# The last pair's row sums of each batch: 32 columns wide, spread by transfers that ACT issues

## The reference

```
xn = group_norm(x)                        # 32 groups
q, k, v = split(w_qkv @ xn + b_qkv)       # 8 heads of 64 channels, 1024 positions
weight = softmax(q.T @ k / sqrt(64))      # over the 1024 keys
a = weight @ v
out = x + w_proj @ a + b_proj
```

## Time and profile before

| | |
|---|---|
| median of 3 runs | 2465.75 us (2464.68 to 2466.75) |
| the profiled execution's own time | 2465.66 us |
| its span | 2464.1 us |
| busy: PE, DVE, ACT, POOL | 2429.1, 1617.7, 1152.5, 1182.9 us |
| granted TensorE clock, mean | 0.994 of full speed |

### The profile page before, as it was taken

One profiled execution on the slowest core, in us unless ns is written; L12 is line 12 of the kernel. 1 busy time (PEld: TensorE's weight loads), 2 busy tenths in 40 slices (PEclk: granted clock), 3 DMA queues, 4 the chain that ended last, 5 costly groups with the idle time before them and its releaser, 6 DMA issues.

```text
span 2464.1 us, 37575 instructions
## 1 busy us (share of the span) xinstructions
PE 2429.1 (99%) x12980; PEld 1611.7 (65%) x12980; DVE 1617.7 (66%) x2164; ACT 1152.5 (47%) x1499; POOL 1182.9 (48%) x590
## 2 busy tenths in 40 slices
PE   8999999999899999999999999999999999999999
PEld 7878888788665566557556655755575566557555
DVE  7555555455566765775677577567756775775677
ACT  3322233223355644654555556456545554562554
POOL 3330000000047665773775567557737666672674
PEclk8999999999899999999999999999999999999999
DMA  6331110112231332315022312422151223222121
GB/s 201 133 113 41 68 68 35 50 51 84 113 112 35 112 128 95 120 35 214 31 98 98 142 36 110 177 71 102 28 213 35 104 100 131 78 69 103 35 69 44
DMA packets 73978, 226.76 MB, mean 92 GB/s; under 512 B 12288, under 2 KB 12288, under 8 KB 72960
## 3 DMA queue, kind: packets, MB, share of 16 engines
q1 hardware_dynamic: 59296, 172.01, 19.8%
q0 software_dynamic: 14560, 52.96, 5.9%
HBM read 141.05 MB, written 71.30 MB: 86 GB/s over the span
## 4 chain that ended last, share of the span: by engine, by line
PE 94%; DVE 3%; POOL 1%; issue 1%; ACT 1%; DMA 0%; ACTq 0%; SPq 0%; DVEq 0%; POOLq 0%
PE psum L1611 18%; PE psum L1551 15%; PE psum L1592 14%; PE psum L1364 11%; PE psum L1383 7%; PE psum L1562 7%; PE psum L1732 7%; PE psum L1407 4%; PE psum L1435 3%; PE psum L1630 2%; PE psum L1481 2%; POOL a_all L612 1%; PE psum L1375 1%; PE psum L1651 1%; PE psum L1495 1%
## 5 line engine op out<-in xcount | busy, mean ns | idle before, releaser
L612 POOL TENSOR_TENSOR a_all<-a_all 128x1024 f32<-128x1024 f32 x410 | 1011.3, 2467 | 496.2 <-ACT a_all L843 461.3
L843 ACT ACTIVATE a_all<-psum 128x1024 f32<-128x1024 f32 x512 | 496.5, 1021 | 79.7 <-PE psum L1592 65.5
L1146 DVE TENSOR_REDUCE small<-psum 128x2 f32<-128x1024 f32 x326 | 398.9, 1226 | 166.8 <-PE psum L1562 166.6
L1611 PE MATMUL psum<-a_all 128*64 128x512 f32 x2048 | 495.7, 605 | 0.0
L1592 PE MATMUL psum<-r_all 64*128 64x512 f32 x3200 | 415.6, 392 | 3.5 <-ACT a_all L843 2.0
L1551 PE MATMUL psum<-r_all 128*128 128x512 f32 x1536 | 364.1, 396 | 4.5 <-DVE r_all L1263 4.5
L1592 PEld LDWEIGHTS psum<-r_all 64*128 64x128 f32 x3200 | 299.8, 185 | 73.2 <-ACT a_all L843 14.0
L1551 PEld LDWEIGHTS psum<-r_all 128*128 128x128 f32 x1536 | 285.5, 189 | 85.1 <-issue 23.3
L1364 PE MATMUL psum<-r_all 128*128 128x512 f32 x1152 | 277.1, 396 | 1.1
L1611 PEld LDWEIGHTS psum<-a_all 128*64 128x64 f32 x2048 | 124.0, 136 | 232.8 <-issue 173.3
L1364 PEld LDWEIGHTS psum<-r_all 128*128 128x128 f32 x1152 | 213.1, 188 | 64.3 <-DVE r_all L1013 10.2
(11 more groups left out here) (157 smaller groups left out, 2613.0 us busy)
## 6 DMA issues: line engine op xcount, KB each, us to landing
r_all<-w_dram SPq DMA_DIRECT2D x48, 1024.0 KB, 4.9
xn_dram<-a_all POOLq DMA_DIRECT2D x56, 512.0 KB, 7.0
r_all<-xn_dram SPq DMA_DIRECT2D x7, 4096.0 KB, 15.4
a_all<-x SPq DMA_DIRECT2D x16, 1024.0 KB, 6.2
y_dram<-a_all SPq DMA_DIRECT2D x16, 1024.0 KB, 4.2
a_all<-y_dram SPq DMA_DIRECT2D x8, 2048.0 KB, 10.8
out<-a_all SPq DMA_DIRECT2D x28, 512.0 KB, 4.1
a_all<-sums SPq DMA_DIRECT2D x192, 64.0 KB, 2.0
```

What stands on the lines that cost most here:

```text
L612: pool.tensor_tensor(to, probs[:, 0, :, cols] if i == 1 else to, probs[:, i % SLOTS, :, cols], ALU.add).then_inc(sum_step, 1)
L843: act.activation(probs[:, i % SLOTS, :, cols], psum[half][:, :, :], ACT.Exp, scale=SCALE).then_inc(probs_ready, 1)
L1146: dve.reduce_max(max2[:, :, tile, half], of[:, :, :], AX_X).then_inc(work_free, 2)
L1611: last = pe.matmul(psum[2][h * D:(h + 1) * D, half], v_t[:, i, head], probs[:, i % SLOTS, h, half * HALF:(half + 1) * HALF], start=(i == 0 ...
```

## The change

The last pair of a batch (of the first seven) goes the way of the other pairs, with two differences. The quarters go to the first bank of psum[1], and the copy stands ahead of the staged row on ACT. And the eight transfers are issued by ACT, on its own queue (`spread_last`), where ACT before had no DMA. Counts of `recip_spread` and `quarters_inverted` now run over four pairs a batch. On DVE the four pieces of reciprocals stand after v tiles 1 and 2, in place of eight after tiles 1 to 4. `normalise` of the last pair waits for the transfers. PE's sums stay between v tiles 1 and 2. The eighth batch's last pair keeps the wide form.

```diff
         def spreads(b, p):
-            return b * (PAIRS - 1) + p
+            return b * PAIRS + p
...
                 act.wait_ge(sums_full, ONE + pairs + 1)
-                if p == PAIRS - 1:
-                    act.wait_ge(o_normed, NORMED0 + pairs * NH)
-                    act.activation(recip, of, ACT.Copy).then_inc(sums_copied, 1)
-                else:
-                    act.wait_ge(recip_spread, ONE + spreads(b, p) * SPREAD)
-                    act.activation(sums4, of, ACT.Copy).then_inc(sums_copied, 1)
+                act.wait_ge(recip_spread, ONE + spreads(b, p) * SPREAD)
+                act.activation(sums4, of, ACT.Copy).then_inc(sums_copied, 1)
+
+            def spread_last(b):
+                p = PAIRS - 1
+                act.wait_ge(quarters_inverted, (spreads(b, p) + 1) * CT)
+                act.wait_ge(o_normed, NORMED0 + (b * PAIRS + p) * NH)
+                for k in range(2 * NH):
+                    for r in range(2):
+                        at = k // NH * D + r * QUARTER
+                        act.dma_start(recip[at:at + QUARTER, k % NH], sums4[k * QUARTER:(k + 1) * QUARTER]).then_inc(recip_spread, 16)
...
                 if not last:
                     for h in range(NH):
                         hid_hi(b, PAIRS - 2, h)
+                    copy_sums(b, PAIRS - 1, psum[1][:, 0])
...
                 else:
-                    copy_sums(b, PAIRS - 1, psum[1][:, :, :])
+                    spread_last(b)
                 for h in range(NH):
                     hid_hi(b, PAIRS - 1, h)
...
                 for piece in range(first, first + n):
-                    if p == PAIRS - 1:
-                        part = recip[:, piece // CT, piece % CT * P:(piece % CT + 1) * P]
-                        dve.reciprocal(part, part).then_inc(sums_inverted, 1)
-                    else:
-                        part = sums4[:, piece * P:(piece + 1) * P]
-                        dve.reciprocal(part, part).then_inc(quarters_inverted, 1)
+                    part = sums4[:, piece * P:(piece + 1) * P]
+                    dve.reciprocal(part, part).then_inc(quarters_inverted, 1)
...
-                if p == PAIRS - 1:
-                    dve.wait_ge(sums_inverted, b * PIECES + (h + 1) * CT)
+                if end:
+                    dve.wait_ge(sums_inverted, h + 1)
                 elif h == 0:
                     dve.wait_ge(recip_spread, ONE + (spreads(b, p) + 1) * SPREAD)
...
-                        if 1 <= i <= 4:
+                        if i in (1, 2):
                             invert_sums(b, PAIRS - 1, 2 * (i - 1), 2)
...
                         if i == 1:
-                            sums(b * PAIRS + PAIRS - 1)
+                            sums(b * PAIRS + PAIRS - 1, psum[1][:, 0])
```

More of the change, by code:

```diff
@@ L321, in build @@
         ADDS = 2 * (NT - 1) - 1
-        PIECES = 2 * CT
         QUARTER = D // 2
@@ L1201, in invert_last, with normalise @@
                     dve.wait_ge(o_normed, NORMED0 + pairs * NH)
-                dve.reciprocal(recip[:, h], psum[1][:, h]).then_inc(sums_inverted, CT)
-            def normalise(b, p, h):
+                dve.reciprocal(recip[:, h], psum[1][:, h]).then_inc(sums_inverted, 1)
+            def normalise(b, p, h, end=False):
                 pairs = b * PAIRS + p
@@ L1327, in batch1 @@
                         invert_last(h)
-                        normalise(b, PAIRS - 1, h)
+                        normalise(b, PAIRS - 1, h, True)
                         hid_lo(b, PAIRS - 1, h)
```

## The result

| | before | after |
|---|---|---|
| median of 5 runs, us | 2464.72 (2464.56 to 2466.75) | 2480.38 (2477.22 to 2483.01) |
| ratio | | 1.0061, 95% interval 1.0049 to 1.0072 |
| profiled execution, us | 2465.66 | 2483.01 (span 2481.5) |

The kernel became slower by 15.7 us, 0.6%. The forecast was 2464.1 with a range to 2471: wrong, and outside its range.

What follows compares the result with a forecast made beforehand. PE's own queue was taken to bound the kernel (94% of the chain). The profiled 2465.66 us less PE's 1.7, other parts costing nothing, gave 2464.0, stated as 2464.1 after the runs' median; range 2460.5 to 2471.

Steps and rivals of the forecast that it cites:

- Landing under load: Last 64 KB transfer beside loaded DMA queues: 2.0 us to land plus 0.7 us loss, bounds 0 and 2.9.
- the issue's price: ACT's eight transfer issues: 0.62 us from one to the next, taken from SP's spreads; last issue at 1125.1.
- deadline of the last landing: Last landing before DVE's final multiplies may be as late as 1129.0 free; past that each microsecond costs PE one.
- T: Time the last of ACT's eight transfers lands at the second batch's end, forecast 1127.8.
- PE's gain: Narrow sums at seven ends save 1.7 us in all, since v tile 0's copy holds v tile 2; bounds 0 and 6.1.
- Rival C: At the sums' switch to full tiles, PE repays the saving by a drain or slow wait release; 2465.7, chance 0.15.
- DVE's saved time: Fewer reciprocals and no wait for ACT's copy: 5.1 us less DVE work per end, none of it PE's.
- ACT's work: Smaller copy ahead of the staged row, plus eight issues in ACT's idle time: staged row some 0.65 us later, cost nothing.
- rival A: Spread lands too late, PE's first projection tile waits for hid_lo; 2470 to 2482; chance 0.13 past 5 us, 0.03 below.
- the prediction's own formula: Net cost of late landings: six times what T exceeds 1129.0, less the 1.7 us won.
- the far bound: ACT's issues at 2.09 us each, as SP's with 4 MB queued: T 1138, loss over 50 us, held for remote.

Runs made afterwards that it cites:

- e6: Kernel after, but POOL's two 512 KB stores and the 512 KB load behind them wait until ACT's eight transfers have landed; 2466.06 us, ratio 1.0002.
- e7: e6 with SP's residual load cut from 2 MB to 512 KB (other rows stale); 2466.08 us, ratio 1.0004.
- e9: Kernel after, but all POOL transfers at a batch's end wait for the spread, the 1 MB load behind the stores; 2468.21 us, ratio 1.0009.
- e10: e6, but SP issues the eight transfers right behind its 2 MB residual load and ACT issues none; 2462.98 us, ratio 0.9990.
- e5: Kernel after, but SP issues the eight transfers ahead of its residual load and ACT issues none; 2487.27 us, ratio 1.0084.
- e2: Kernel after, but SP's residual load brings 512 KB instead of 2 MB (three quarters stale); 2488.58 us, ratio 1.0090.
- e1: Kernel before, with only PE's last-pair sums in the 32-column form (divisors then wrong); 2464.67 us, ratio 0.9996.
- e3: Kernel after, but POOL's 1 MB load is issued behind the wait for its first row's stores; 2499.64 us, ratio 1.0133.
- e11: e6, but SP issues the seventh end's transfers behind its residual load, ACT those of the six ends in the loop; 2465.83 us, ratio 1.0000.
- e8: Kernel after, but only POOL's 512 KB load behind the stores waits for the spread; the stores go at once; 2479.80 us, ratio 1.0063.

## Why the prediction was wrong

**The step that failed: "Landing under load" with the issue's price ahead of it.** The mechanism, a deadline of the last landing, was right; the price was not. With the shift of 1.33 us taken off, the first issue came at 1120.8, as forecast. The last issue started 6.87 us after the first (1129.01 - 1122.14), where 7 x 0.62 = 4.34 were taken: 2.5 us. The last landing took 2.92 us where 2.7 were taken: 0.2 us. T was 1130.6, 2.8 us past the forecast. Nearly all of it lies in the issues, and I had put the whole loss under load into the landing. The prediction held the 0.62 us because SP's issues are steady in the earlier trace rows; but none of those 192 transfers runs while POOL has one under way. A price was taken from a quiet place for a busy one.

The landing's own 2.7 us came nearly right by luck. I had added 0.7 us for load to the 2.0 us of the earlier trace rows. But the last of the eight takes as long without POOL's stores: 2.7 to 3.6 us at the seven ends of e6, e7, e9 and e10, and 3.07 at the seventh end of the kernel after, where nothing of SP or POOL is under way. During each of these landings a 16 KB packet of the queue that the profile names "instruction" (q8) is under way, as in the window from 1129 to 1130 below. During the last landing of SP's other spreads, which take 2.0 us, there is none. So that packet is the likely cause; no run moves it.

**What sets that price** is shown by the stores' own test: as they wait, eight issues go from 8.28 to 5.03 us and the six gaps from 12.2 us to one of 0.2 (e6); on SP's queue it is the same (7.05 in e5, 4.95 in e10); the loads alone stretch no issue (e6, e7, e9). That the two fall together could have been seen. In the kernel before, POOL's first store is issued right behind its subtraction of the staged row; the prediction moved that row by 0.65 us and put ACT's first issue at 1120.8, but gave no time for the stores. They are issued 0.1 us after ACT's first transfer.

How the DMA engines come to do this is seen only in part. Queue by queue (packets, MB, share of 16 engines; q0 is POOL's, q1 SP's, q10 ACT's) in the kernel after, first from 1122 to 1125, then from 1126 to 1127, then from 1129 to 1130:

```profile
q0 software_dynamic: 146, 0.60, 53.5%
q1 hardware_dynamic: 141, 0.57, 50.1%
...
q0 software_dynamic: 110, 0.39, 94.3%
q10 hardware_dynamic: 33, 0.03, 9.8%
...
q10 hardware_dynamic: 132, 0.18, 62.6%
q8 instruction: 1, 0.02, 5.8%
q0 software_dynamic: 11, 0.02, 4.4%
```

While POOL's stores run, ACT's queue moves 0.03 MB in a microsecond, and 0.18 as soon as they are through. In e6 it moves 0.22 MB from 1123 to 1124. Ahead of that, from 1122 to 1125, it moves nothing, though three transfers are issued.

Its first packet comes 3.4 us after the first issue, as SP's load ends. In e6 it is 3.0 us, again as that load ends. In e9, where SP's load has nothing of POOL beside it and ends early, it is 1.2, and in e2, where only POOL's stores are under way, 1.4. So the loads do delay the first landings (the median over all eight is 2.0 us in e9, 3.2 in e6, 3.6 in the kernel after), but not the last one, on which DVE waits.

The prediction quoted the Trainium skill (DMA: Bandwidth & Descriptors, "Queues, rings and completion order"), by which each engine takes turns between the queues a packet at a time, and T would be near 1127.8. The trace agrees for POOL's and SP's queues, 146 packets against 141. For the third queue it does not: none for 3.4 us, then 33 against 110, and T was 1130.6.

Why the issues stretch stays open. That the queue is full is not the reason for the third one: in e6, too, nothing of the queue has moved for 3.0 us, and the four issues that end by then take 0.54 to 0.62 us each. The first long issue, the third, starts as POOL's second store has just been issued (1123.35 against 1122.83 + 0.53). Whether it is stores, or any transfer that POOL issues just then, no run tells apart.

**The deadline** held. At the second end T lay at 1131.95 and the gap was 1.74, so the deadline was at 1130.2, which is 1128.9 with the shift of 1.33 taken off (forecast 1129.0). Each microsecond past it cost about one (this end: 2.0 us more than in e6, for a gap of 1.74), and more where the clock fell.

**PE's gain was right in size, and one reason given for it was not.** Where the landing is in time the seven ends gain 1.6 us (e6) and 1.9 (e10), for 1.7 forecast. The weight load follows v tile 0's copy, and the wait that the sums had covered now stands on PE as 0.53 us of idle time. Rival C's drain in the open is therefore out: with it e6 would gain nothing. But the prediction says of DVE's saved time that none of it is PE's. e1 shows that this is so only while PE is late: made earlier by 0.3 us, PE needs v tile 2's copy earlier as well, and gets it only if DVE's wait of 1.42 us and its long reciprocals are gone. Of the 1.7 us, the narrow form brings 0.8, and the rest needs the lighter DVE.

**ACT's work "cost nothing".** At the ends that held. The stall in the seventh batch was in no rival. It is 1.77 us or absent in the kernels whose ACT issues no transfers (before, e1, e5, e10), and 3.9 to 4.2 in all those in which it does (after, e2, e3, e6 to e9, e11). By the timelines it costs 5.1 us in the kernel after and 3.8 in e6; e6 and e10, which differ in the queue of the spread, lie 2466.06 - 2462.98 = 3.1 us apart (on two chips).

The DMA queues say what ACT most likely waited for. The queue named "instruction" with packets of 8 KB (q14) is silent in the kernel before from 861 to 2110 us, while the batches run in the loop, and has its next packets behind it. The kernel after from 2117 to 2119, from 2119 to 2120, then the kernel before from 2110 to 2111:

```profile
q1 hardware_dynamic: 204, 0.84, 101.8%
...
q1 hardware_dynamic: 29, 0.05, 13.8%
q14 instruction: 1, 0.01, 1.9%
...
q14 instruction: 1, 0.01, 2.7%
```

In all eleven kernels with a stall it ends 1.5 us after the first of these packets starts. In the three with 1.77 us the packet starts 0.3 us into the stall, on idle DMA engines. In the eight with 3.9 us or more it starts 2.4 to 2.7 us into it. SP's 1 MB load of weights, issued just before, fills the engines up to that moment (102% of 16 in the row above), and the packet moves as soon as the load is through. Read so, ACT waits for its own instructions. With the DMA issues in its loop it needs the next piece at an earlier place, where it collides with that load. That is inferred from the traces; no run shifts the load or pads the code. What the stall costs also hangs on the granted clock: 2.9 us by the timelines in e7, whose clock stays at 1.00 behind it, 3.8 in e6 with 3.4 us at 0.50, and 5.1 in the kernel after with 6.8 us at 0.50.

**The range** left out the far part of rival A, because both of its bounds, 0.9 us an issue and 2.9 us of loss on the landing, had to come together. They did not come together: the landing lost 0.9 us. The issue alone crossed the line, since its bound was too low: 6.87 / 7 = 0.98 us from one to the next, with single issues of up to 2.05. With T at 1130.6 the prediction's own formula gives 6 x 1.6 - 1.7 = +7.9 us, 2473.6, past the range already. What lies between this and 2480 it did not have: the late fifth end with its fall of the clock, and the stall. So the nearness to 2482 was luck. The error in the chances was a bound for the issue that came from no row; the far bound that did, 2.09 us an issue, was held for remote, and single issues met it.

The sum on profiled executions: 2465.66 + 13.3 at the ends + 5.1 at the stall - 0.5 ahead of the first end = 2483.6, beside 2483.01 measured. The 0.6 us left over I haven't followed.

## What to carry to other kernels

Before a small transfer goes on a path with a deadline, list what every other queue issues in the same microseconds, with the change's own shifts applied; a duration from a stretch where those queues are idle is no price for one where they store. Take a rival's bound from a row too, or it bounds nothing. And a change that puts the first DMA issues on an engine should be timed against the same change on a queue that already issues them, with a look at where the loads of instructions fall in both.

## What the runs showed of the hardware

- Two 512 KB stores of GpSimd that start with eight 64 KB transfers within SBUF stretch the issues of these from 5.0 us for eight to between 6.8 and 8.7, on ACT's queue and on SP's alike. The last landing they leave as it is (2.5 to 3.6 us in the kernel after, 2.7 to 3.6 where they wait). Loads of 2 MB and 1 MB from HBM that were issued first stretch no issue; with them the median landing is 3.2 us (e6), with SP's load alone 2.0 (e9).
- While SP's 2 MB load was under way beside POOL's transfers, ACT's queue moved its first packet only as that load ended, 3.0 us (e6) and 3.4 us (after) after its first issue; beside POOL's stores alone it was 1.4 us (e2), with neither 1.2 (e7).
- A load of POOL that is issued half a microsecond before the last of the eight comes with a later landing of it: 3.8 us in e2 and 6.0 in e3 at the second end. In e8, with that load away, it took 3.3.
- ACT's issue of a 64 KB transfer costs about what SP's does, 0.61 us against 0.59, where nothing disturbs it.
- ACT stalled once behind its loop, and went on 1.5 us after a packet of the queue named "instruction" had started: the stall took 1.77 us where that packet met idle DMA engines, 3.9 to 4.2 us where a 1 MB load filled them.
- Behind 3.64 us of idle PE at the fifth end the granted clock was 0.50 for 3.4 us; behind the gaps of 1.55 to 1.89 us at the other five ends with a gap it stayed at 1.00.
